# A GNN kernel whose opening is issued in another order, with two node tiles normalised by VectorE instead of ScalarE

## The chip, the cores and the metric

The kernel runs on one core of a Trainium2 chip. The metric is the device time of one execution in microseconds (us); smaller is better. The core's engines work side by side and meet at semaphores: TensorE (PE in the rows; PEld is its weight load), VectorE (DVE), ScalarE (ACT), GpSimd (POOL) and SyncE (SP), which here only issues transfers. An engine name with a q behind it (SPq, ACTq) is that engine's own sequencer, issuing a transfer. Each engine works off its own queue strictly in the order in which the program wrote it.

## What is computed

Four residual graph layers over N = 384 nodes with 1024 features. Each begins with the same step, and only the beginning of the first layer and the end of the last are touched here:

```python
h = jnp.maximum(_layernorm(x, axis=-1), 0.0)
x = x + attention(h, edges, edge_type_5)        # q = x @ wq.T + bq, k, v; q2 = q @ wiq.T + biq, ...; masked softmax
h = jnp.maximum(_layernorm(x, axis=-1), 0.0)
x = x + relational_conv(h, edges, edge_type_8)  # gated, 8 relations
h = jnp.maximum(_layernorm(x, axis=-1), 0.0)
x = x + sage(h, src, dst)                       # two layers
h = jnp.maximum(_layernorm(x, axis=-1), 0.0)
x = x + (h @ W.T + bias)                        # W scattered from (dst, src, edge_weight): 384 columns in use
```

`_layernorm(x)` is (x - mean) / sqrt(var + 1e-5). The mask of the attention comes from the 6144 edges: each (src, dst, type) writes a softplus of one of four edge weights into a 384 x 384 table, the last one winning.

## The kernel before

Nodes lie in NT = 3 tiles of P = 128 rows, features in KT = 8 blocks of 128. All products are made in split precision: each fp32 operand is turned into a high part (ScalarE's copy to fp32r, semaphores with "hi") and a low part (what is left, by VectorE's or GpSimd's subtraction, semaphores with "lo"), and each product is three matmuls. Everything is ordered by hand: each engine's block lists its instructions one by one, with waits on named semaphores.

The opening. SyncE loads the three tiles of x (`xres`, L280; semaphores x_part) and then the pieces of the first four tiles of wq (`raw`, L332). ScalarE issues the loads of src, dst and the two edge types (`e_in`, L903; semaphore edges_in, 16 for each). VectorE takes the statistics of each node tile: two bn_stats of 512 columns (L1262), then their aggregate (L1266). ScalarE takes the square root (`norm_std`, L910), VectorE the reciprocal and the shift -mean/std (`norm_shift`, L1275, L1276), and ScalarE normalises and applies the relu in one instruction (`norm_relu_0`, L933) into `h0`, with its columns permuted to go with the weights. `START` (L219) lists the work as (tile, first block, last block): tile 0, tile 1, and tile 2 in two halves. TensorE transposes each (L488) into PSUM, ScalarE reads it into the high part of `acts` (`start_high`, L941), VectorE makes the low part (`start_low`, L1355).

In between, VectorE makes four rows of the edges in `e_row` (L1289 to L1295): the key src * N + dst, its transpose, the type, and the key with the relation. The last one (L1295) gives `edge_rows`, for which SyncE waits to store the key rows (`rows_d`, L341) and to gather them broadcast to all partitions (`rows_b`, L285), and for which TensorE waits to turn them (`turn_edges`, L426) into PSUM bank 0; VectorE copies them out (`e_col`, L1363), and TensorE waits for that before it uses the bank again. GpSimd fills constants, then issues six loads of biases (`b_in`, L1789), which TensorE turns in one go (L493) and ScalarE copies (`bcol`, L998). Three small VectorE instructions (L1298 to L1300, `sp`) prepare the softplus, which ScalarE's L993 and L995 go on with.

The weights come by VectorE's transpose of 32 x 32 blocks (`turn_tile`, L1333, into `xres`, which is free by then), ScalarE's high part (`tile_high`, L954), and VectorE's low part (`tile_low`, L1337); weight tile 0's low part alone is made by GpSimd (L1794). A column tile (`column_tile`, L476) is 24 matmuls of 384 columns. It waits for its weight's low part, the first one also for `start_lo` up to 3 (tile 2's first half) and 4, and from the third on for the output two tiles before it to be read out of PSUM: high part L1005 by ScalarE, low part L1400 by VectorE (`out_lo`). Ahead of each L1400 VectorE makes two key comparisons (`meet`, L1310), which read the gathered rows.

The tail. In the last layer each node tile's sum is finished (L1735), its statistics taken, and it is normalised over its first 384 columns by ScalarE (L916), transposed by TensorE (L443), split (L926, L1325), and multiplied (nine matmuls, L892). VectorE adds the result to `u` (L1765), which GpSimd has made of x and the bias (L1946), and SyncE stores it.

## Time and profile before

| | us |
|---|---|
| median of 3 runs | 928.15 |
| lowest and highest | 927.82, 928.22 |
| the profiled execution | 927.87 |
| its span, first to last instruction | 926.1 |
| busy in the span: TensorE, VectorE, GpSimd, ScalarE | 906.8, 611.5, 492.3, 359.2 |

All rows are of the one profiled execution, with times in us from the start of its span. In a timeline a row is the start, how long it was busy, the engine, the line of the kernel, the operation, output <- inputs with partitions x elements, and a count where several were merged; behind it, in brackets, how long the engine sat idle before it and what released it. The granted clock of TensorE was 0.996 of full speed over the span. TensorE is busy nearly all the time, so the places to look at are those where it isn't yet, or not any more, fed without a gap: the first 29 us and the last 10.

### The profile page before, as it was taken

To read this page: it belongs to the slowest core of one execution; us is meant where nothing else is said; L and a number is where in the kernel's file an instruction comes from. 1 tells how busy PE (TensorE), PEld (TensorE's weight loads), DVE (VectorE), ACT (ScalarE), POOL (GpSimd) and SP (SyncE) were. 2 spreads that over 40 slices of the span, in tenths; PEclk is the share of its full clock that TensorE was granted. 3 is DMA by queue.
4 is the path that set the end of the run, shared out by engine and by line. 5 is a ranking of instruction groups with operands and counts; after the bars stand their busy time and mean duration, and the time that the engine had idled before them with its cause. 6 is when DMAs were issued, how large, how long until landed. Compare 5 with 4: busy or idle time off the path is not lost.

```text
span 926.1 us, 13755 instructions
## 1 busy us (share of the span) xinstructions
PE 906.8 (98%) x4787; PEld 799.0 (86%) x4787; DVE 611.5 (66%) x993; ACT 359.2 (39%) x558; POOL 492.3 (53%) x436
## 2 busy tenths in 40 slices
PE   4999999999999999999999999999999999999998
PEld 4999999998888888888888888888888878888886
DVE  6998888896996735665656565565656565434545
ACT  6433333345885343223223223232325235224422
POOL 5334446775765515757657575756686402220463
PEclk8999999999999999999999999999999999999999
DMA  8998756634336644344554444444333534323412
GB/s 207 241 277 224 229 155 151 167 85 119 53 52 204 178 155 146 92 151 114 152 152 130 153 113 150 113 148 111 97 91 137 182 98 154 114 93 91 140 42 91
DMA packets 89907, 128.60 MB, mean 139 GB/s; under 512 B 34480, under 2 KB 67456, under 8 KB 89856
## 3 DMA queue, kind: packets, MB, share of 16 engines
q1 hardware_dynamic: 72784, 123.54, 43.8%
q0 software_dynamic: 15552, 0.11, 4.0%
q10 hardware_dynamic: 1520, 4.30, 1.4%
q8 instruction: 29, 0.48, 0.2%
q14 instruction: 22, 0.18, 0.1%
HBM read 117.17 MB, written 7.59 MB: 135 GB/s over the span
## 4 chain that ended last, share of the span: by engine, by line
PE 90%; DVE 3%; ACT 2%; POOL 1%; DMA 1%; issue 1%; POOLq 0%; DVEq 0%; ACTq 0%
PE ps L682 49%; PE ps L476 17%; PE ps L756 9%; PE ps L520 4%; PE ps L645 4%; PE ps L600 2%; PE ps L543 2%; PE ps L556 2%; DMA weight_d<-weight_sum,cell 1%; PE ps L435 1%; POOL weight_d L1890 1%; PE ps L892 1%; DVE wlo_all L1388 1%; POOL mean_lo L1869 0%; PE ps L443 0%
## 5 line engine op out<-in xcount | busy, mean ns | idle before, releaser
L1388 DVE TENSOR_TENSOR wlo_all<-raw,whi_all 128x1024 fp32r<-128x1024 f32 x120 | 200.4, 1681 | 119.6 <-ACT whi_all L972 118.5
L476 PE MATMUL ps<-acts,whi_all 128*128 128x384 f32 (+1 forms) x640 | 164.1, 337 | 0.8 <-DVE acts L1400 0.6
L1869 POOL TENSOR_TENSOR mean_lo<-mean_f,mean_hi 128x384 fp32r<-128x384 f32 x76 | 88.3, 1162 | 120.4 <-ACT mean_hi L1124 120.4
L1124 ACT ACTIVATE mean_hi<-mean_f 128x384 fp32r<-128x384 f32 x76 | 39.9, 525 | 277.2 <-DVE mean_f L1562 277.2
L682 PE MATMUL ps<-whi_all,mean_hi 128*128 128x512 f32 x452 | 139.5, 390 | 0.3 <-POOL mean_lo L1869 0.3
L682 PE MATMUL ps<-wlo_all,mean_hi 128*128 128x512 f32 x452 | 139.3, 389 | 0.0
L682 PE MATMUL ps<-whi_all,mean_lo 128*128 128x512 f32 x452 | 139.3, 389 | 0.0
L972 ACT ACTIVATE whi_all<-raw 128x1024 fp32r<-128x1024 f32 x120 | 125.1, 1050 | 32.0 <-PE ps L682 28.5
L476 PEld LDWEIGHTS ps<-acts,whi_all 128*128 128x128 f32 x640 | 116.8, 190 | 1.2 <-DVE acts L1400 0.9
L1890 POOL DMA_INDIRECT weight_d<-weight_sum,cell x48 | 95.5, 1989 | 30.4 <-DMA weight_d<-weight_sum,cell 17.5
L476 PE MATMUL ps<-acts,wlo_all 128*128 128x384 f32 (+1 forms) x320 | 107.6, 336 | 0.0
L1833 POOL DMA_INDIRECT count_d<-met,cell x48 | 81.3, 1693 | 45.2 <-DMA count_d<-met,cell 32.0
L682 PEld LDWEIGHTS ps<-whi_all,mean_lo 128*128 128x128 f32 x452 | 84.9, 188 | 17.7
L682 PEld LDWEIGHTS ps<-wlo_all,mean_hi 128*128 128x128 f32 x452 | 84.9, 188 | 17.6
L682 PEld LDWEIGHTS ps<-whi_all,mean_hi 128*128 128x128 f32 x452 | 83.8, 188 | 12.6 <-issue 0.7
L1820 POOL DMA_INDIRECT mask_d<-type_val,cell x48 | 52.8, 1100 | 68.1 <-DMA mask_d<-type_val,cell 58.1
L1562 DVE TENSOR_TENSOR mean_f<-ps,inv 128x384 f32<-128x384 f32 x76 | 42.1, 554 | 60.5 <-PE ps L756 59.1
L1864 POOL TENSOR_TENSOR h_row_lo<-h,h_row_hi 128x1024 fp32r<-128x1024 f32 x9 | 24.6, 2756 | 99.1 <-ACT h_row_hi L1119 99.1
L756 PE MATMUL ps<-rel_r,h_row_lo 128*128 128x384 f32 x192 | 64.9, 338 | 0.0
L756 PE MATMUL ps<-rel_r,h_row_hi 128*128 128x384 f32 x192 | 64.9, 338 | 0.0
L1005 ACT ACTIVATE acts<-ps,bcol 128x384 f32 x40 | 23.3, 582 | 100.7 <-PE ps L476 87.9
L682 PE MATMUL ps<-whi_all,h_t_hi 128*128 128x512 f32 x192 | 60.8, 398 | 0.6 <-DVE wlo_all L1388 0.5
(211 smaller groups left out, 1705.6 us busy)
## 6 DMA issues: line engine op xcount, KB each, us to landing
raw<-in_L_gnn_weight SPq DMA_DIRECT2D x64, 512.0 KB
rows_b<-rows_d SPq DMA_DIRECT2D x24, 384.0 KB, 4.8
raw<-in_L_gnn_w_gate SPq DMA_DIRECT2D x16, 512.0 KB
raw<-in_L_gnn_W_self SPq DMA_DIRECT2D x16, 512.0 KB
raw<-in_L_gnn_W_neigh SPq DMA_DIRECT2D x16, 512.0 KB
count_d<-total_r SPq DMA_DIRECT2D x8, 576.0 KB
rel_r<-count_d SPq DMA_DIRECT2D x8, 576.0 KB, 4.5
raw<-in_L_gnn_wq SPq DMA_DIRECT2D x32, 128.0 KB
```

Source lines behind the costliest of these rows:

```text
L476: mm = pe.matmul(ps[:, j % 2, 0:N], stationary[j % RING][:, k, :], acts[:, a, moving, k, :], start=i == 0, stop=i == 3 * KT - 1)
L520: mm = pe.matmul(ps[:, V_BANK[n % 4], 0:V_COLS].rearrange("p (j o) -> p j o", j=2), acts[:, 3, a, k, P * nt:P * nt + P], weight[:, slots, ...
L682: mm = pe.matmul(ps[:, 2 * nt + f, :], stationary[a][:, k, P * nt:P * nt + P], weight[slot][:, HALF * f:HALF * f + HALF], start=first and ...
L756: mm = pe.matmul(ps[:, 7 - k % 2, 0:N], h_row[a][:, s, P * k:P * k + P], edges[:, s, :], start=i == 0, stop=i == 2 * NT - 1)
L972: act.activation(whi_row[slot], raw[slot][:, :], ACT.Copy).then_inc(S["w_hi"], 1)
L1124: act.activation(mean_of(q, k, 0)[:, 0, :], sums_of(q, k), ACT.Copy).then_inc(S["mean_hi"], 1)
L1388: dve.tensor_tensor(wlo_row[slot], raw[slot][:, :], whi_row[slot].bitcast(F32), ALU.subtract)\
L1562: dve.tensor_tensor(sums_of(q, k), ps[:, 7 - k % 2, 0:N], inv[:, :], ALU.mult)\
L1820: pool.indirect_dma_start(mask_d, bass.IndirectOffsetOnAxis(ap=cell[:, 0, c:c + 1], axis=0), type_val[:, c:c + 1], None).then_inc(mask_sca ...
L1833: pool.indirect_dma_start(count_d, bass.IndirectOffsetOnAxis(ap=cell[:, 1, c:c + 1], axis=0), met[:, 1, c:c + 1], None, compute_op=ALU.add)\
L1869: pool.tensor_tensor(mean_of(q, k, 1)[:, 0, :], sums_of(q, k), mean_of(q, k, 0)[:, 0, :].bitcast(F32), ALU.subtract).then_inc(S["mean_lo"], 1)
L1890: pool.indirect_dma_start(weight_d, bass.IndirectOffsetOnAxis(ap=cell[:, 2, c:c + 1], axis=0), weight_sum[:, c:c + 1], None, compute_op=AL ...
```

## The change

The opening, engine by engine:

- SyncE loads tile 0 of x in two halves of 512 columns, the first with a semaphore of its own, `x_half`.
- The four edge fields signal two semaphores, `ends_in` (src, dst) and `edges_in` (the types).
- VectorE takes each tile's stats as soon as its piece has landed, and does `norm_shift` of tile nt between the two halves of the stats of tile nt + 1. The two keys that need only src and dst are made behind tile 0's stats; the type row and the key with the relation (`edge_types`) only behind the low part of tile 0. Edge columns and the softplus's three small instructions are moved behind the last low part.
- Tile 2 is normalised by VectorE (`start_norm`, one tensor_scalar for each half, without the relu). The relu is applied where the transposed tile is read from PSUM: ScalarE's high part uses Relu for Copy, VectorE's low part is max(x, 0) - high in one scalar_tensor_tensor.
- ScalarE takes tile 2's square root ahead of tile 0's high part and has no normalisation of tile 2.
- TensorE turns the edges only after all node tiles, into bank 2 beside the biases, and doesn't wait for the edge columns any more; ScalarE does, before it copies `bcol`.
- GpSimd issues the six bias loads behind its first two instructions instead of behind its fills.

In the tail the last node tile is normalised by VectorE in the same way: a tensor_scalar of 384 columns, Relu for Copy in the high part, and max and subtract in the low part.

How the queues stand now. VectorE in the opening, from the shift of node tile 2 to the second weight transpose (L1333 or L1349), before (L1293 and L1295 make the type row and the key with the relation, L1363 the edge columns, L1298 to L1300 the softplus's first steps):

```order
L1276 TENSOR_SCALAR shift<-mv,rstd 128x1
L1293 CAST e_row<-e_in 48x128
L1295 SCALAR_TENSOR_TENSOR e_row<-e_in,e_row 48x128
L1298 TENSOR_SCALAR sp<-etw_b 128x4
L1299 TENSOR_SCALAR sp<-etw_b 128x4
L1300 TENSOR_TENSOR sp<-etw_b,sp 128x4
L1333 STREAM_TRANSPOSE xres<-raw 128x1024
L1355 TENSOR_TENSOR acts<-ps,acts 128x8x128
L1363 COPY e_col<-ps 128x192
L1355 TENSOR_TENSOR acts<-ps,acts 128x8x128
L1355 TENSOR_TENSOR acts<-ps,acts 128x4x128 x2
L1333 STREAM_TRANSPOSE xres<-raw 128x1024
```

and after (L1297 is the new normalisation, L1376 the low parts of tile 2; L1373 is L1355 of before):

```order
L1276 TENSOR_SCALAR shift<-mv,rstd 128x1
L1297 TENSOR_SCALAR h<-xres,rstd,shift 128x4x4x32 x2
L1373 TENSOR_TENSOR acts<-ps,acts 128x8x128
L1289 CAST e_row<-e_in 48x128
L1291 SCALAR_TENSOR_TENSOR e_row<-e_in,e_row 48x128
L1373 TENSOR_TENSOR acts<-ps,acts 128x8x128
L1376 SCALAR_TENSOR_TENSOR acts<-ps,acts 128x4x128 x2
L1391 COPY e_col<-ps 128x192
L1394 TENSOR_SCALAR sp<-etw_b 128x4
L1395 TENSOR_SCALAR sp<-etw_b 128x4
L1396 TENSOR_TENSOR sp<-etw_b,sp 128x4
L1349 STREAM_TRANSPOSE xres<-raw 128x1024
```

The type row and the key moved behind the low part of tile 0, the edge columns and the softplus behind all low parts, and the first weight transpose ahead of the shift.

ScalarE in the opening, from the first normalisation (L933, now L935) on; L910 (L912) is the square root, L941 (L943) a high part of a node tile, L954 (L956) one of a weight tile. Before:

```order
L933 ACTIVATE h<-xres,shift,rstd 128x4x8x32
L910 ACTIVATE std<-mv,epsc 128x1
L933 ACTIVATE h<-xres,shift,rstd 128x4x8x32
L941 ACTIVATE acts<-ps 128x8x128
L910 ACTIVATE std<-mv,epsc 128x1
L933 ACTIVATE h<-xres,shift,rstd 128x4x4x32 x2
L954 ACTIVATE whi_all<-xres 128x1024
L941 ACTIVATE acts<-ps 128x8x128
L941 ACTIVATE acts<-ps 128x4x128 x2
L954 ACTIVATE whi_all<-xres 128x1024
```

After:

```order
L935 ACTIVATE h<-xres,shift,rstd 128x4x8x32
L912 ACTIVATE std<-mv,epsc 128x1
L935 ACTIVATE h<-xres,shift,rstd 128x4x8x32
L912 ACTIVATE std<-mv,epsc 128x1
L943 ACTIVATE acts<-ps 128x8x128
L956 ACTIVATE whi_all<-xres 128x1024
L943 ACTIVATE acts<-ps 128x8x128
L943 ACTIVATE acts<-ps 128x4x128 x2
L956 ACTIVATE whi_all<-xres 128x1024
```

The normalisations of tile 2 are gone and its square root stands ahead of tile 0's high part.

VectorE in the tail, from the aggregate of the last tile's stats on, before:

```order
L1266 BN_AGGR mv<-stats 128x2
L1325 TENSOR_TENSOR h_t_lo<-ps,h_t_hi 128x3x128
L1275 RECIPROCAL rstd<-std 128x1
L1276 TENSOR_SCALAR shift<-mv,rstd 128x1
L1325 TENSOR_TENSOR h_t_lo<-ps,h_t_hi 128x3x128
L1765 TENSOR_TENSOR u<-u,ps 128x384 x3
```

and after:

```order
L1266 BN_AGGR mv<-stats 128x2
L1341 TENSOR_TENSOR h_t_lo<-ps,h_t_hi 128x3x128
L1275 RECIPROCAL rstd<-std 128x1
L1276 TENSOR_SCALAR shift<-mv,rstd 128x1
L1790 TENSOR_SCALAR h<-xres,rstd,shift 128x384
L1794 SCALAR_TENSOR_TENSOR h_t_lo<-ps,h_t_hi 128x3x128
L1802 TENSOR_TENSOR u<-u,ps 128x384 x3
```

The normalisation (L1790) has come in behind the shift, and the low part has become one scalar_tensor_tensor.

The diff, cut to its core:

```diff
@@ sync
-            for nt in range(NT):
+            sp_.dma_start(xres[:, 0, 0:HALF], x_rows[:, 0, 0:HALF]).then_inc(x_half, 16)
+            sp_.dma_start(xres[:, 0, HALF:D], x_rows[:, 0, HALF:D]).then_inc(x_part[0], 16)
+            for nt in range(1, NT):
                 sp_.dma_start(xres[:, nt, :], x_rows[:, nt, :]).then_inc(x_part[nt], 16)
@@ tensor
-                if n == 2:
-                    turn_edges()
...
+            pe.wait_ge(S["start_lo"], 1)
+            turn_edges()
             pe.wait_ge(S["bcol_in"], 16 * 6)
-            pe.wait_ge(S["start_lo"], 1)
             pe.transpose(ps[:, 2, 0:6 * KT], b_in[:, :], ident[0:6 * KT, 0:6 * KT]).then_inc(S["bcol_made"], 1)
-            pe.wait_ge(S["edge_cols"], 1)
@@ scalar
-                act.activation(acts[:, 0, 0, k0:k1, P * nt:P * nt + P], start_block(nt, k0, k1), ACT.Copy)\
-                   .then_inc(S["start_hi"], 1)
+                act.activation(acts[:, 0, 0, k0:k1, P * nt:P * nt + P], start_block(nt, k0, k1),
+                               ACT.Copy if nt < NT - 1 else ACT.Relu).then_inc(S["start_hi"], 1)
...
             norm_relu_0(*START[1])
+            norm_std(0, 2)
             start_high(0)
-            norm_std(0, 2)
-            norm_relu_0(*START[2])
-            norm_relu_0(*START[3])
             tile_high(0, 0)
...
             norm_std(3, 2)
-            norm_relu(3, 2, h, FIRST_THIRD)
-            tile_turned_high(Y_H3 + 2, 2, NT)
+            tile_turned_high(Y_H3 + 2, 2, NT, ACT.Relu)
@@ vector
+            def start_norm(nt, k0, k1):
+
+                dve.wait_ge(S["shift_ready"], nt + 1)
+                dve.tensor_scalar(h0[:, nt, :].rearrange("p (f b i) -> p b f i", f=KT, b=4)[:, :, k0:k1],
+                                  xres[:, nt, :].rearrange("p (b f i) -> p b f i", f=KT, b=4)[:, :, k0:k1],
+                                  rstd[:, nt, :], shift[:, nt, :], ALU.mult, ALU.add).then_inc(S["h_ready"], 1)
+
+            dve.wait_ge(x_half, 16)
+            half_stats(0, 0)
+            dve.wait_ge(x_part[0], 16)
+            half_stats(0, 1)
+            var_of(0, 0)
+            edge_keys()
+            dve.wait_ge(x_part[1], 16)
+            half_stats(1, 0)
+            norm_shift(0, 0)
+            half_stats(1, 1)
+            var_of(0, 1)
+            dve.wait_ge(x_part[2], 16)
+            half_stats(2, 0)
+            norm_shift(0, 1)
+            half_stats(2, 1)
+            var_of(0, 2)
...
             turn_tile(0, 0)
+            norm_shift(0, 2)
+            start_norm(*START[2])
+            start_norm(*START[3])
             start_low(0)
-            dve.wait_ge(S["edges_turned"], 1)
-            dve.tensor_copy(e_col[:, :, :], ps[:, 0, 0:4 * EC].rearrange("p (f c) -> p f c", f=4))\
-               .then_inc(S["edge_cols"], 1)
+            edge_types()
             start_low(1)
             start_low(2)
             start_low(3)
+            dve.wait_ge(S["edges_turned"], 1)
+            dve.wait_ge(S["bcol_made"], 1)
+            dve.tensor_copy(e_col[:, :, :], ps[:, 2, P:P + 4 * EC].rearrange("p (f c) -> p f c", f=4))\
+               .then_inc(S["edge_cols"], 1)
...
-            tile_turned_low(Y_H3 + 2, 2, NT)
+            dve.wait_ge(S["shift_ready"], NT * 4)
+            dve.tensor_scalar(h[:, NT - 1, 0:N], xres[:, NT - 1, 0:N], rstd[:, NT - 1, :], shift[:, NT - 1, :],
+                              ALU.mult, ALU.add).then_inc(S["h_ready"], 1)
...
@@ gpsimd
+            for g, b in enumerate((bq, bk, bv, biq, bik, biv)):
+                pool.dma_start(b_in[KT * g:KT * g + KT, :].rearrange("j (c o) -> j c o", c=4) if g < 3
...
             pool.memset(total_r[:, :, :].bitcast(F32), 0.0).then_inc(S["zeros_made"], 1)
```

## Rows read from the trace of the kernel before

**Rows 1.** Engines' busy time over the span, from the page: us, share, instructions.
```profile
PE 906.8 (98%) x4787; PEld 799.0 (86%) x4787; DVE 611.5 (66%) x993; ACT 359.2 (39%) x558; POOL 492.3 (53%) x436
```

**Rows 2.** VectorE in the timeline of the opening: start us, us, engine, line, operation.
```profile
8.72 1.28 DVE L1262 BATCH_NORM_STATS2 stats<-xres 128x6 f32<-128x512 f32 x2
...
11.69 0.28 DVE L1295 SCALAR_TENSOR_TENSOR e_row<-e_in,e_row 48x128 f32<-48x128 int32 x1
11.89 0.15 DVE L1298 TENSOR_SCALAR sp<-etw_b 128x4 f32<-128x4 f32 x1
...
12.38 1.25 DVE L1333 STREAM_TRANSPOSE xres<-raw 128x1024 f32<-128x1024 f32 x1
...
13.55 1.19 DVE L1355 TENSOR_TENSOR acts<-ps,acts 128x1024 fp32r<-128x1024 f32 x1
...
14.66 0.34 DVE L1363 COPY e_col<-ps 128x192 f32<-128x192 f32 x1
...
15.66 2.42 DVE L1355 TENSOR_TENSOR acts<-ps,acts 128x1024 fp32r<-128x1024 f32 x3 [0.66 <-ACT acts L941]
...
17.99 1.24 DVE L1333 STREAM_TRANSPOSE xres<-raw 128x1024 f32<-128x1024 f32 x1
```

**Rows 3.** ScalarE and GpSimd in the same timeline.
```profile
8.84 1.24 ACT L933 ACTIVATE h<-xres,shift,rstd 128x1024 f32<-128x1024 f32 x1 [0.48 <-DVE shift L1276]
...
9.99 1.02 ACT L941 ACTIVATE acts<-ps 128x1024 fp32r<-128x1024 f32 x1
...
13.66 1.06 ACT L954 ACTIVATE whi_all<-xres 128x1024 fp32r<-128x1024 f32 x1 [0.46 <-DVE xres L1333]
...
14.80 2.36 POOL L1794 TENSOR_TENSOR wlo_all<-xres,whi_all 128x1024 fp32r<-128x1024 f32 x1 [4.59 <-ACT whi_all L954]
...
17.12 1.01 POOL L1799 TENSOR_TENSOR moved<-e_col,spare 128x48 f32<-128x48 f32 x3
```

**Rows 4.** Timelines of TensorE and VectorE, first and third column tile.
```profile
17.63 0.98 PE L476 MATMUL ps<-acts,whi_all 128*128 128x384 f32 x2 [0.21 <-DVE acts L1355]
...
27.90 0.61 DVE L1400 SCALAR_TENSOR_TENSOR acts<-ps,bcol,acts 128x384 fp32r<-128x384 f32 x1
...
28.57 0.61 PE L476 MATMUL ps<-acts,whi_all 128*128 128x384 f32 x2 [0.57 <-DVE acts L1400]
```

**Rows 5.** Tile view of xres, transfers: ns and start; time to landing.
```profile
L280 SPq DMA_DIRECT2D xres<-in_x x3: 394/415/424, 0.8 to 1.7; - x3
...
DMA to landing us min/median/max: 3.4/4.4/6.7
```

**Rows 6.** Timeline at 702 of GpSimd and VectorE; L1388's durations.
```profile
701.84 2.40 POOL L1930 TENSOR_TENSOR rows_b<-rows_b,h 128x1024 f32<-128x1024 f32 x1 [7.14 <-DMA brow<-in_L_gnn_b_gate]
...
702.16 3.17 DVE L1388 TENSOR_TENSOR wlo_all<-raw,whi_all 128x1024 fp32r<-128x1024 f32 x1 [2.09 <-ACT whi_all L972]
...
L1388 DVE TENSOR_TENSOR wlo_all<-raw,whi_all x120: 1171/1226/3908, 311.9 to 899.2; 128x1024 fp32r<-128x1024 f32 x120
```

**Rows 7.** Timeline of the tail, all engines.
```profile
917.26 2.40 POOL L1946 TENSOR_TENSOR u<-xres,brow 128x1024 f32<-128x1024 f32 x1 [1.99 <-DVE xres L1735]
...
918.71 0.21 DVE L1276 TENSOR_SCALAR shift<-mv,rstd 128x1 f32<-128x1 f32 x1
...
918.96 0.71 ACT L916 ACTIVATE h<-xres,shift,rstd 128x384 f32<-128x384 f32 x1 [0.48 <-DVE shift L1276]
919.08 0.68 PE L892 MATMUL ps<-w_hi,h_t_lo 128*128 128x384 f32 x3
...
919.72 0.55 PE L443 MATMUL ps<-ident,h 128*128 128x128 f32 x3
```

**Rows 8.** SyncE's key rows: timeline; transfers with size and time to landing.
```profile
11.99 0.31 SPq L341 DMA_DIRECT2D rows_d<-e_row  x1
...
rows_b<-rows_d SPq DMA_DIRECT2D x3, 384.0 KB, 5.0
...
rows_d<-e_row SPq DMA_DIRECT2D x1, 48.0 KB, 6.2
```

More of the change, by code:

```diff
@@ L425, in turn_edges @@
                 for f in range(4):
-                    mm = pe.transpose(ps[:, 0, EC * f:EC * f + EC], e_row[:, f, :], ident[0:EC, 0:EC])
+                    mm = pe.transpose(ps[:, 2, P + EC * f:P + EC * f + EC], e_row[:, f, :], ident[0:EC, 0:EC])
                 mm.then_inc(S["edges_turned"], 1)
@@ L1277, in norm_shift @@
                    .then_inc(S["shift_ready"], 1)
-            def start_stats(nt):
-                dve.wait_ge(x_part[nt], 16)
-                norm_stats(0, nt)
-            for nt in range(NT):
-                start_stats(nt)
-                if nt < NT - 1:
-                    norm_shift(0, nt)
-            dve.wait_ge(S["edges_in"], 16 * 4)
-            dve.scalar_tensor_tensor(e_row[:, KEY, :], e_in[:, 0, :], float(N), e_in[:, 1, :], ALU.mult, ALU.add)\
-               .then_inc(S["key_made"], 1)
@@ L1291, in _ @@
-            dve.scalar_tensor_tensor(e_row[:, KEY_T, :], e_in[:, 1, :], float(N), e_in[:, 0, :], ALU.mult, ALU.add)
-            norm_shift(0, NT - 1)
-            dve.tensor_copy(e_row[:, TYPE, :], e_in[:, 3, :])
-            dve.wait_ge(S["key_made"], 1)
-            dve.scalar_tensor_tensor(e_row[:, REL_KEY, :], e_in[:, 2, :], float(N * N), e_row[:, KEY, :],
-                                     ALU.mult, ALU.add).then_inc(S["edge_rows"], 1)
-            dve.wait_ge(S["etw_in"], 16)
-            link(dve.tensor_scalar(sp[:, 0, :], etw_b[:, :], 0.0, None, ALU.max))
@@ L1299, in _, with edge_keys @@
-            link(dve.tensor_scalar(sp[:, 1, :], etw_b[:, :], -1.0, None, ALU.mult))
-            dve.tensor_tensor(sp[:, 2, :], etw_b[:, :], sp[:, 1, :], ALU.max).then_inc(S["sp_max"], 1)
+            def edge_keys():
+                dve.wait_ge(S["ends_in"], 16 * 2)
+                dve.scalar_tensor_tensor(e_row[:, KEY, :], e_in[:, 0, :], float(N), e_in[:, 1, :], ALU.mult, ALU.add)\
+                   .then_inc(S["key_made"], 1)
+                dve.scalar_tensor_tensor(e_row[:, KEY_T, :], e_in[:, 1, :], float(N), e_in[:, 0, :], ALU.mult, ALU.add)
@@ new lines, in edge_types @@
+            def edge_types():
+                dve.wait_ge(S["edges_in"], 16 * 2)
+                dve.tensor_copy(e_row[:, TYPE, :], e_in[:, 3, :])
+                dve.wait_ge(S["key_made"], 1)
+                dve.scalar_tensor_tensor(e_row[:, REL_KEY, :], e_in[:, 2, :], float(N * N), e_row[:, KEY, :],
+                                         ALU.mult, ALU.add).then_inc(S["edge_rows"], 1)
+            def start_norm(nt, k0, k1):
[3 more added lines that the diff above has]
+                                  rstd[:, nt, :], shift[:, nt, :], ALU.mult, ALU.add).then_inc(S["h_ready"], 1)
@@ L1354, in start_low @@
                 dve.wait_ge(S["start_hi"], n + 1)
[L1355 to L1357 removed]
+                low, high = [acts[:, 0, a, k0:k1, P * nt:P * nt + P] for a in (1, 0)]
+                if nt < NT - 1:
+                    dve.tensor_tensor(low, start_block(nt, k0, k1), high.bitcast(F32), ALU.subtract)\
+                       .then_inc(S["start_lo"], 1)
+                else:
+                    dve.scalar_tensor_tensor(low, start_block(nt, k0, k1), 0.0, high.bitcast(F32), ALU.max,
+                                             ALU.subtract).then_inc(S["start_lo"], 1)
             dve.wait_ge(S["h_ready"], 1)
             turn_tile(0, 0)
+            norm_shift(0, 2)
+            start_norm(*START[2])
+            start_norm(*START[3])
             start_low(0)
[L1362 to L1364 removed]
+            edge_types()
             start_low(1)
```

32 lines of the change are left out of this document (20 added, 12 removed).

## The prediction

> **What bounds the kernel now.** I read the page's first part first: TensorE is busy 98% of the span [rows 1]. In such a kernel a change to the opening or to the tail counts only through the moment from which TensorE never waits again, and through what follows its last matmul. So I looked next for TensorE's last long wait in the opening. It is the third column tile of the first projection: its first matmul starts at 28.57 after 0.57 us of idle time, released by VectorE's L1400, which started at 27.90 [rows 4]. TensorE had begun its first column tile at 17.63 [rows 4], so an earlier beginning of that tile alone only makes the 0.57 us of waiting longer. What counts is the chain of VectorE from the second weight transpose (17.99, [rows 2]) to that L1400. I call the start of that transpose T. All that stands between T and L1400 (two more transposes, two low parts, the softplus of the edge weights by way of ScalarE, the mask blocks, two key comparisons) is in the same order before and after, so L1400 moves with T, one to one. This holds as long as TensorE ends its second column tile, 0.57 us ahead of the wait, before L1400 is there.
>
> The tail is a single chain as well: shift of node tile 2 on VectorE, normalisation on ScalarE (0.71 us), transposes on TensorE, and the last nine matmuls [rows 7].
>
> **Part 1, x in halves and the stats in another order.** Three transfers of x are issued at 0.8 to 1.7; their times to landing are 3.4, 4.4 and 6.7 us, so tile 2 lands at about 1.7 + 6.7 = 8.4 [rows 5]. Before, VectorE reaches tile 2's stats at 8.72 [rows 2] and finds them landed. In the new order VectorE does tile 0 by about 5.2, the two key rows (some 0.45), tile 1 by about 7.6, and then waits for tile 2. So what half a tile of x gains is lost at once to the landing of tile 2; I take 8.43 for the start of its stats (0.3 earlier than before). It could be 0.4 later, since one more issue of 0.42 stands ahead of it [rows 5], or a little sooner; the whole opening then moves with it.
>
> Behind the first half of the stats (0.6) come reciprocal and shift of tile 1 (0.4), now at 9.44, where before ScalarE could start on that tile at 8.84 [rows 3]. So ScalarE normalises tile 1 at 9.5, 0.6 later. It then has the square root of tile 2 (10.65, since L941 follows L933 by 1.15), the high part of tile 0 (10.85 to 11.85, its 1.02) and the high part of weight tile 0 at 11.85 to 12.9, in place of 13.66 to 14.72 [rows 3]. That is the gain of this part: ScalarE no longer normalises tile 2 ahead of the weight. GpSimd's low part of weight tile 0 (2.36) follows at 12.95 and ends at 15.3, where before it ran from 14.80 to 17.16 [rows 3].
>
> **Part 2, VectorE between there and T.** After the last stats (10.3): transpose 1.17 from its start to the next [rows 2], reciprocal and shift 0.4, so 11.85; the two halves of tile 2, normalised. No row shows a tensor_scalar of 512 elements from SBUF to SBUF; the bounds are 0.27 (half of the stats' 0.6, less what is fixed in it) and 0.60 (the spacing of the 512-element stats [rows 2]). It doesn't matter which, as will be seen. They end at 12.4 to 13.0. Low part of tile 0 (1.19 [rows 2]): to 13.5 or 14.1. And then comes the moved part: the cast of the types and the key with the relation (e_row<-e_in,e_row). Before, these ran at 11.69 [rows 2], with GpSimd idle. Now they come at 13.5 to 14.1, in the middle of GpSimd's low part of the weight (12.95 to 15.3). That key instruction reads two operands in SBUF, as GpSimd's does. What such a pair does is seen at 702: VectorE's L1388, also with two SBUF operands, starts at 702.16, takes 3.17 us (their median is 1.23) and ends 1.1 us after GpSimd's L1930 has ended at 704.24 [rows 6]. It waited for GpSimd's instruction to end. I expect the same here: the key instruction starts at 15.3, and all of VectorE's queue stands behind it (the low parts of tiles 1 and 2, the edge columns, the softplus, T). The Trainium skill says the same, in SBUF — State Buffer, section "Who interferes with whom": a VectorE instruction with two SBUF inputs contends with a GpSimd one that reads SBUF, and the second blocks wholly; by that rule, which the row at 702 bears out, the sum stays as it is.
>
> From there: key 0.2, low part of tile 1 from 15.5, then 1.13 and twice 0.6 (15.66 to 17.99 before, [rows 2]), which gives 17.85. Then the two pieces that used to stand ahead: edge columns 0.3, and the three small softplus instructions 0.49 (11.89 to 12.38, [rows 2]): T = 18.65. The softplus ones now run beside GpSimd's three L1799 (1.01 in all, starting right behind the edge columns; [rows 3]). They may wait for each other: 0 to 0.6, and I take 0.2. T = 18.85 against 17.99: **0.85 us later**. The low part of tile 2's first half ends at about 17.3, so TensorE starts its column tile at 17.4 instead of 17.6, which buys nothing.
>
> **Part 3, the b_in transfers issued first, and turned edges in bank 2.** GpSimd's six issues move ahead of its fills, which end later by as much, still before its low part of the weight can start; the first to read a fill is VectorE, behind T. The biases, issued some microseconds sooner, are no longer the last to arrive. Cost and gain nothing; their cover is that VectorE's low parts end last. The turned edges (0.5 us of TensorE) now follow the key at 15.6 and are ready at 16.3, with the bias transpose at 16.6; VectorE wants them at 17.85. If TensorE were 1.2 us later there, this would begin to cost.
>
> **Part 4, the tail.** Before: shift ends 918.92, ScalarE normalises 918.96 to 919.67, TensorE transposes at 919.72 [rows 7]. TensorE itself is busy with tile 1's product: its last group of three starts at 919.08 at 0.17 each [rows 7], so it could take the transposes at 919.6 and no sooner. The new VectorE instruction (384 elements) would be ready at 918.96 and take 0.27 to 0.46, so the gain is capped at 0.12. The other bound: GpSimd's L1946 runs from 917.26 to 919.66 [rows 7]. If VectorE waits for it as at 702, it starts at 919.6 and ends at 919.9 to 920.1, a loss of 0.2 to 0.4. No row shows a VectorE instruction with one SBUF operand beside a long one of GpSimd; the nearest that shows anything is the elementwise L1388, which waits. I take that side: **+0.25**. The Trainium skill (same page, same section) lists tensor_scalar among the operations that can use both ports and so contend with GpSimd; by it the tail would lose, and without it gain 0.12. The relu is done while reading PSUM, at the price of the copy. TensorE's nine last matmuls and the store are the same.
>
> **Sum.** +0.85 + 0.25 = +1.1 us. The profiled execution took 927.87, which gives 929.0; the median of the runs is 0.28 above it, and on that base I predict **929.2**. That is 0.12%, below the 0.2% (1.9 us) that a measurement of this kernel can tell from no change.
>
> **Rivals.**
> *No wait in the opening*: the key instruction (48 partitions only) passes beside GpSimd. Then the low part of tile 1 starts when ScalarE's high part of it is there, 13.85, or up to 14.3 with the slower normalisation, and T = that + 3.15 = 17.0 to 17.45: 0.55 to 1.0 us earlier. TensorE's own chain, begun 0.9 or more earlier too, does not take its place. With the tail at -0.1 to +0.25: 927.0 to 927.9, likeliest 927.4. For it: it is a third as many partitions and an eighth as many elements as L1388, and no row shows so small a one beside a long one of GpSimd. Against it: the row at 702. Chance 0.27.
> *Slower by more than 0.2%*: the stored key rows. SyncE stores them at 11.99, it takes 6.2 us to land, and the gather behind it 5.0 [rows 8]. Now the store can't be issued before 15.6; if it still takes 6.2, the gather is issued at 21.9 and lands at 26.9; the first comparison, one of two that take 0.9 together right ahead of L1400 (27.90, [rows 4]), was at 27.0 and is due at 27.9. The margin is 1.0. For it: the whole SyncE queue, raw tiles too, stands behind. Against: before, the store waited behind sixteen weight pieces on its queue, and those are nearly done at 15.6. If the gather took 7 instead of 5, the comparison would be 1.0 late: 929.2 + 1.0 = 930.2; the gather at 7.5 gives 930.7. Chance 0.11.
> *Faster by more than 0.2%*: needs no wait in the opening and tile 2 of x a full microsecond sooner. Chance 0.04.
>
> **How the numbers follow.** The forecast has 0.58, with its own range 928.6 to 929.9 (tile 2 of x 0.4 later; softplus 0 to 0.6; tail from -0.1 to +0.4). No wait 0.27, slower 0.11, faster 0.04. The range 926.9 to 930.3 holds the forecast, the no-wait case and the near part of the slow one. Faster 0.04, same 0.84, slower 0.12.
>
> **What would show it.** VectorE's stats of tile 2 wait for the transfer until 8.4; GpSimd's low part of the weight runs from 13.0 to 15.3; the key or the cast before it shows a duration of 1 to 2 us and ends at 15.3 to 15.6; the second weight transpose starts at 18.6 to 19.3; TensorE idles 1.3 us or more ahead of its third column tile, released by the same product at 29.2 to 29.7; the VectorE normalisation at 918.9 ends only after GpSimd's addition. I am wrong if the key shows 0.28 us, or if the second transpose starts before 17.9, or if the first comparison waits for a transfer.

## The result, and the profile after

The changed kernel takes **932.58 us** (median of 7 runs, lowest 932.28), the kernel before 927.85 (median of 7 runs beside them): ratio 1.0058, 95% interval [1.0044, 1.0073]. Slower by 0.58%, outside the predicted range (926.9 to 930.3), whose middle case was 929.2. The profiled execution of the changed kernel took 932.28, its span is 930.5 against 926.1. Of most kernels here, the one before included, some executions take 2 to 9 us longer than the rest, so medians are compared.

VectorE, ScalarE and GpSimd in the timeline of the opening of the changed kernel (start us, us, engine, line, operation; in brackets the idle time before and what ended it). Its lines are numbered up to 37 higher than those of the kernel before. The rows answer to [rows 2, 3]:

```profile
9.04 0.69 DVE L1262 BATCH_NORM_STATS2 stats<-xres 128x6 f32<-128x512 f32 x1 [2.91 <-DMA xres<-in_x]
...
11.38 0.69 DVE L1262 BATCH_NORM_STATS2 stats<-xres 128x6 f32<-128x512 f32 x1 [0.49 <-DMA xres<-in_x]
...
14.09 1.25 DVE L1349 STREAM_TRANSPOSE xres<-raw 128x1024 f32<-128x1024 f32 x1 [0.86 <-DMA raw<-in_L_gnn_wq]
...
15.66 1.01 DVE L1297 TENSOR_SCALAR h<-xres,rstd,shift 128x512 f32<-128x512 f32 x2
...
17.72 1.26 DVE L1289 CAST e_row<-e_in 48x128 f32<-48x128 int32 x1
18.90 0.28 DVE L1291 SCALAR_TENSOR_TENSOR e_row<-e_in,e_row 48x128 f32<-48x128 int32 x1
...
22.27 1.25 DVE L1349 STREAM_TRANSPOSE xres<-raw 128x1024 f32<-128x1024 f32 x1
...
15.37 1.06 ACT L956 ACTIVATE whi_all<-xres 128x1024 fp32r<-128x1024 f32 x1 [0.61 <-DVE xres L1349]
...
16.51 2.39 POOL L1831 TENSOR_TENSOR wlo_all<-xres,whi_all 128x1024 fp32r<-128x1024 f32 x1 [5.83 <-ACT whi_all L956]
21.85 1.03 POOL L1836 TENSOR_TENSOR moved<-e_col,spare 128x48 f32<-128x48 f32 x3 [2.96 <-DVE e_col L1391]
```

Three things are to be seen. The statistics of node tile 1 (9.04) and of tile 2 (11.38) wait for their transfers, 2.91 and 0.49 us. The first weight transpose (14.09) waits 0.86 for its tile. And the cast of the types, 0.21 us before, lasts from 17.72 to 18.98, until GpSimd's low part of the weight (16.51 + 2.39 = 18.90) has ended. The second weight transpose, T, starts at 22.27 in place of 17.99: **4.28 us later**.

TensorE's waits in the opening and the last row of the tail (answering to [rows 4, 7]):

```profile
21.05 0.98 PE L479 MATMUL ps<-acts,whi_all 128*128 128x384 f32 x2 [0.99 <-DVE acts L1376]
...
32.85 0.62 PE L479 MATMUL ps<-acts,whi_all 128*128 128x384 f32 x2 [0.66 <-DVE acts L1429]
...
32.19 0.60 DVE L1429 SCALAR_TENSOR_TENSOR acts<-ps,bcol,acts 128x384 fp32r<-128x384 f32 x1
...
921.46 2.40 POOL L1983 TENSOR_TENSOR u<-xres,brow 128x1024 f32<-128x1024 f32 x1 [1.99 <-DVE xres L1764]
...
922.91 0.21 DVE L1276 TENSOR_SCALAR shift<-mv,rstd 128x1 f32<-128x1 f32 x1
...
923.16 0.92 DVE L1790 TENSOR_SCALAR h<-xres,rstd,shift 128x384 f32<-128x384 f32 x1
...
924.71 0.49 ACT L928 ACTIVATE h_t_hi<-ps 128x384 fp32r<-128x384 f32 x1 [2.04 <-PE ps L446]
```

The product that releases the third column tile starts at 32.19 instead of 27.90: 4.29 later, as T. In the tail the normalisation of 384 elements lasts 0.92 us beside GpSimd's L1983, and from the shift's start to the high part pass 1.80 us, where it was 1.60 in the kernel before (918.71 [rows 7] to 920.31, its row below): +0.2. The two together are 4.5; the span grew by 4.4.

```profile
920.31 0.49 ACT L926 ACTIVATE h_t_hi<-ps 128x384 fp32r<-128x384 f32 x1 [0.64 <-PE ps L443]
```

### The profile page after: what moved, and what is told of

Its sections match the earlier page's. It is cut to its first block, busy times and chain, and to the rows that moved or that the text cites. A ratio compares the mean times of both kernels' runs of the same rounds, so it can differ in the third digit from the quotient of the medians.

```text
span 930.5 us, 13757 instructions
## 1 busy us (share of the span) xinstructions
PE 908.6 (98%) x4787; PEld 800.6 (86%) x4787; DVE 613.7 (66%) x996; ACT 357.0 (38%) x555; POOL 493.5 (53%) x436
## 4 chain that ended last, share of the span: by engine, by line
PE 89%; DVE 4%; DMA 2%; ACT 1%; POOL 1%; issue 1%; SPq 0%; DVEq 0%; POOLq 0%; ACTq 0%
PE ps L683 49%; PE ps L479 17%; PE ps L757 9%; PE ps L521 4%; PE ps L646 4%; PE ps L601 2%; PE ps L544 2%; PE ps L557 2%; DMA raw<-in_L_gnn_wq 1%; DMA weight_d<-weight_sum,cell 1%; PE ps L438 1%; POOL weight_d L1927 1%; DVE wlo_all L1417 1%; POOL mean_lo L1906 0%; PE ps L467 0%
## 5 line engine op out<-in xcount | busy, mean ns | idle before, releaser
L1857 POOL DMA_INDIRECT mask_d<-type_val,cell x48 | 56.0, 1166 | 65.6 <-DMA mask_d<-type_val,cell 55.6
```

The source lines that it names most:

```text
L1857: pool.indirect_dma_start(mask_d, bass.IndirectOffsetOnAxis(ap=cell[:, 0, c:c + 1], axis=0), type_val[:, c:c + 1], None).then_inc(mask_sca ...
```

## The experiments

All runs stand against 21 to 35 runs of the kernel before, 927.92 to 927.96 in the median. T is read from each profile; between two profiles of one opening it differed by 0.48 us (`a_whole` and its second look, 19.97 and 19.49) and by 0.11 (`a_types` and `a_types_fill`, 20.22 and 20.11). The three suspects in the opening are tile 0 of x in two transfers, the bias loads ahead of GpSimd's fills, and the place of the casts.

### First four: the transfers

`a_bin_late`, the changed kernel with the bias loads back behind the fills:

```diff
-            for g, b in enumerate((bq, bk, bv, biq, bik, biv)):   # ahead of memset(total_r)
...
+            for g, b in enumerate((bq, bk, bv, biq, bik, biv)):   # ahead of wait_ge(S["w_hi"], 1)
```

> The changed kernel with one part undone: GpSimd's six bias loads issued behind its fills, as before. Theory A (the early bias loads disturb the x loads, whose second and third tile landed 3 us late): the stats of tile 1 start by 6.0 and those of tile 2 at 8.4 to 8.8; the waits on GpSimd's low part stay, so the time is 929.0 to 929.8. Theory B (x in two halves is what delays the tiles): no change, 932.3 to 932.8, tile 2's stats at 11.4.

`a_whole`, tile 0 of x in one transfer again:

```diff
-            sp_.dma_start(xres[:, 0, 0:HALF], x_rows[:, 0, 0:HALF]).then_inc(x_half, 16)
-            sp_.dma_start(xres[:, 0, HALF:D], x_rows[:, 0, HALF:D]).then_inc(x_part[0], 16)
-            for nt in range(1, NT):
+            for nt in range(NT):
```

> The changed kernel with tile 0 of x loaded whole again, the bias loads still early. Theory A: as the changed kernel, 932.3 to 932.8, tile 2's stats at 11.0 to 11.4. Theory B: tile 1's stats by 6.0, tile 2's at 8.4, time 929.0 to 929.8.

`a_both`, both edits at once:

> The changed kernel with both undone: tile 0 of x whole and the bias loads behind the fills. Both theories: x as in the kernel before (tile 2's stats at 8.4 to 8.7); what is left over the kernel before is the waiting of VectorE for GpSimd's low part of the weight (0.85 us forecast) and the tail (0.2): 928.9 to 929.4. If the whole excess were the transfers': 927.9 or less.

`b_bin_early`, the kernel before with the bias loads ahead of the fills:

> The kernel before with one part of the change alone: the six bias loads issued ahead of GpSimd's fills. Theory A: tile 1's stats start near 9 and tile 2's near 11.4, and the time rises by 2 to 3 us, to 930 to 931. Theory B: 927.8 to 928.2, as before.

Measured, with T and the span of the profiled execution:

| kernel | median us | ratio, 95% interval | T | span |
|---|---|---|---|---|
| before | 927.96 | | 17.99 | 926.1 |
| a_bin_late | 931.81 | 1.0044 [1.0027, 1.0061] | 21.04 | 929.4 |
| a_whole | 932.4, see below | 1.0047 [1.0030, 1.0064] | 19.97 | 928.4 |
| a_both | 929.89 | 1.0036 [1.0021, 1.0051] | 19.14 | 927.5 |
| b_bin_early | 927.97 | 1.0000 [0.9990, 1.0009] | 18.09 | 926.4 |

VectorE in the timeline of `a_bin_late`:

```profile
8.26 0.69 DVE L1262 BATCH_NORM_STATS2 stats<-xres 128x6 f32<-128x512 f32 x1 [2.42 <-DMA xres<-in_x]
...
10.88 0.69 DVE L1262 BATCH_NORM_STATS2 stats<-xres 128x6 f32<-128x512 f32 x1 [0.77 <-DMA xres<-in_x]
...
12.72 1.25 DVE L1349 STREAM_TRANSPOSE xres<-raw 128x1024 f32<-128x1024 f32 x1
```

and in that of `a_whole`:

```profile
6.01 0.68 DVE L1260 BATCH_NORM_STATS2 stats<-xres 128x6 f32<-128x512 f32 x1
...
8.75 0.69 DVE L1260 BATCH_NORM_STATS2 stats<-xres 128x6 f32<-128x512 f32 x1 [0.91 <-DMA xres<-in_x]
...
11.78 1.25 DVE L1346 STREAM_TRANSPOSE xres<-raw 128x1024 f32<-128x1024 f32 x1 [1.19 <-DMA raw<-in_L_gnn_wq]
```

With the halves kept, tiles 1 and 2 still come late (8.26, 10.88); with tile 0 in one transfer tile 1 is there at 6.01 and tile 2 at 8.75. The bias loads are not the cause of that. They may be a smaller one: without them at the front T is 1.23 earlier with the halves kept and 0.83 (against the second profile 0.35) with x whole, and the first weight tile is there sooner (transpose at 12.72 without a wait, against 14.09 with 0.86). The 1.23 is more than T's own scatter and agrees with the times (931.81 against 932.58). With x whole the difference is within the scatter, and both kernels take about 929.6 apart from their long executions, so there it isn't shown. In the kernel before, where VectorE comes to that tile only at 12.38 [rows 2], they change nothing.

`a_both` showed a second thing, in the timelines of VectorE and GpSimd:

```profile
5.63 0.23 DVE L1280 SCALAR_TENSOR_TENSOR e_row<-e_in 48x128 f32<-48x128 int32 x1
5.79 1.24 DVE L1282 SCALAR_TENSOR_TENSOR e_row<-e_in 48x128 f32<-48x128 int32 x1
...
4.45 1.06 POOL L1819 MEMSET mask<- 128x1152 f32 x1
5.58 1.30 POOL L1820 TENSOR_SCALAR_AFFINE_SELECT mask<-mask 128x1152 f32<-128x1152 f32 x1
```

The key's second instruction, 0.28 us in the changed kernel and beside a memset, takes 1.24 us beside GpSimd's affine_select, which reads SBUF, and ends 0.15 us behind it. The first one (5.63) started only 0.05 us behind the affine_select and wasn't held: it took its usual 0.23, and the affine_select 1.30 where it takes 1.16 in the kernel before. The key's wait costs little here, since tile 2's statistics start at 8.71, as in `a_whole` (8.75). The 929.89 lie above the 928.9 to 929.4 that both theories gave; four of its nine runs are long ones (931.35 and more), the other five lie between 929.28 and 929.89.

### Next four: one part alone

`b_halves`, the kernel before with nothing but tile 0 of x in two transfers:

```diff
-            for nt in range(NT):
+            sp_.dma_start(xres[:, 0, 0:HALF], x_rows[:, 0, 0:HALF]).then_inc(x_half, 16)
+            sp_.dma_start(xres[:, 0, HALF:D], x_rows[:, 0, HALF:D]).then_inc(x_part[0], 16)
+            for nt in range(1, NT):
                 sp_.dma_start(xres[:, nt, :], x_rows[:, nt, :]).then_inc(x_part[nt], 16)
```

> The kernel before with one edit: tile 0 of x comes in two transfers, its stats wait for both. Theory 'halves delay the tiles behind them': tiles 1 and 2 of x land about 3 us later (stats of tile 2 at 11 instead of 8.72 us), T from 17.99 to 20.3 or later, time 930.3 or more, ratio 1.0025 or more. Rival 'it needs the changed order too' (the delay in the changed kernel came from the other loads of the opening and chance): stats of tile 2 at 8.7 to 9.3, time 927.9 to 928.4.

Measured: **930.39 us**, 1.0017 [1.0004, 1.0031], T = 20.71, 2.72 later; span 928.8 (+2.7). VectorE's timeline:

```profile
9.25 1.29 DVE L1265 BATCH_NORM_STATS2 stats<-xres 128x6 f32<-128x512 f32 x2 [2.18 <-DMA xres<-in_x]
...
11.49 1.29 DVE L1265 BATCH_NORM_STATS2 stats<-xres 128x6 f32<-128x512 f32 x2
...
20.71 1.23 DVE L1338 STREAM_TRANSPOSE xres<-raw 128x1024 f32<-128x1024 f32 x1
```

Tile 1's statistics start at 9.25 after 2.18 us of waiting, tile 2's at 11.49 in place of 8.72 [rows 2]. The theory stands, in the kernel before as well: the halves alone cost 2.4 us of median.

Two things about it can be read from the traces. The core's 16 DMA engines moved less in the first microseconds: from 3 to 5 us they ran at 404 GB/s in the kernel before, at 208 in `b_halves` and at 245 in the changed kernel; over all profiles it is 391 to 406 with tile 0 in one transfer and 208 to 286 with halves. The rates in 40 slices of 0.65 us from 0 to 26, first of the kernel before, then of the changed one:

```profile
GB/s 0 0 32 191 407 404 415 359 323 333 232 79 137 275 301 232 228 227 226 223 219 225 229 227 199 151 43 0 0 85 288 169 301 295 213 169 252 407 350 217
GB/s 0 0 22 236 378 309 80 301 349 314 379 240 144 300 222 207 249 224 230 246 210 252 199 254 214 178 61 22 22 0 30 46 0 47 269 154 293 281 224 164
```

And tile 2 was overtaken: by the start of its statistics 1.95 MB had been moved in the kernel before (8.72 us at 224 GB/s) and 2.49 MB in the changed one (11.38 at 219), so by this estimate some 0.5 MB more of other loads went first, weight pieces queued behind it for the most part (edges and biases together are 0.12 MB). Whether the shorter rows (2 KB instead of 4) or the additional transfer is the reason was not tested.

`a_types`, the changed kernel with the casts moved right behind the last variance:

```diff
             half_stats(2, 1)
             var_of(0, 2)
+            edge_types()
...
             start_low(0)
-            edge_types()
```

> The changed kernel with the cast of the edge types and their relation key alone moved right behind the last variance (13.2 us in its profile, where VectorE waited 0.86 us for the weight tile, so that they cost nothing there). Theory 'two parts that add up': x in halves keeps its 2.6 us, GpSimd's wait of 1.38 us (17.72 to 19.10) goes: T from 22.27 to 20.9, time 932.58 - 1.4 = 931.2 us, ratio 1.0035. Rival 'the wait hides behind something else', for instance ScalarE's high part of tile 1, which ended at about 17.2: T stays at 22 or above, time 932.2 to 932.6.

`a_both_types`, the same move on top of `a_both`:

> The changed kernel with tile 0 of x in one transfer, the bias loads back behind GpSimd's fills, and the casts of the edge types with their relation key moved right behind the last variance, ahead of GpSimd's low part of the weight. The same without that last move started the second weight transpose (T) at 19.14, with the cast of 1.39 us inside GpSimd's 2.36 us. Theory 'GpSimd makes VectorE wait': cast 0.2 us, low part of tile 1 directly behind that of tile 0, T = 19.14 - 1.52 + 0 = 17.6, third column tile 0.3 earlier than in the kernel before, tail +0.2: 927.8 us, ratio 0.9998. Rival 'the low part of tile 1 is bound by ScalarE's high part anyway': T stays above 18.5, time 928.9 or more. Second question, open: the two runs with x whole scattered by up to 5 us; if this comes from TensorE's clock rising late (it begins the first column tile late after a broken row of short transposes), it goes on here or shrinks with T; if from the cast and what it delays, it is gone and all runs lie within 0.5 us.

Measured: `a_types` 931.47 us, 1.0033 [1.0017, 1.0049], T = 20.22; `a_both_types` 929.04 us, 1.0015 [0.9999, 1.0031], T = 18.92. In `a_types` the cast is back at its size:

```profile
12.86 0.16 DVE L1289 CAST e_row<-e_in 48x128 f32<-48x128 int32 x1
...
13.41 1.25 DVE L1350 STREAM_TRANSPOSE xres<-raw 128x1024 f32<-128x1024 f32 x1 [0.19 <-ACT h L935]
...
20.22 1.25 DVE L1350 STREAM_TRANSPOSE xres<-raw 128x1024 f32<-128x1024 f32 x1
```

T is 2.05 earlier: 1.38 from the cast, 0.68 from the first weight transpose, which starts sooner in this execution (13.41 instead of 14.09). The time fell by 1.1 and the span by 0.4 only. In `a_both_types` the move brought 0.22 instead of 1.52, and neither theory had the reason. The first weight transpose starts at 11.23 instead of 10.81, and above all: with the bias loads late, VectorE's edge columns now wait 0.79 for TensorE's transpose of the biases, which waited 2.17 for b_in.

```profile
18.05 0.36 DVE L1388 COPY e_col<-ps 128x192 f32<-128x192 f32 x1 [0.79 <-PE ps L493]
...
17.61 0.34 PE L493 MATMUL ps<-ident,b_in 48*128 48x48 f32 x1 [2.17 <-DMA b_in<-in_L_gnn_biv]
```

So the two moves of the change depend on each other: early casts need early biases. The second question of that expectation got a plain answer: the scatter went on without the wait (928.62 to 933.39).

`b_tail`, the kernel before with the change of the tail alone (the ScalarE and VectorE lines of the tail in the diff above):

> The kernel before with the change of the tail alone: node tile 2 of the last norm normalised by VectorE, relu while reading PSUM. Theory 'VectorE waits for GpSimd's addition': the normalisation of 384 elements lasts until GpSimd's 2.40 us instruction has ended, from shift to high part 1.59 us instead of 1.39, time 927.96 + 0.2 = 928.2 us, ratio 1.0002. Rival 'the end of the kernel is timed by something else': no difference, 927.96. Rival 'the scatter of the changed kernel comes from the tail': runs here scatter by 1 us and more; by the first theory they lie within 0.5 us.

Measured: 928.23 us against 927.96, 1.0011 [0.9992, 1.0030]: the 0.2 us can't be told from nothing by the ratio, the median sits where it was expected, and the profile has the 0.92 us again. That all runs would lie within 0.5 us was wrong: three of eleven took 931.03, 932.63 and 934.89.

### Last four: what was left over

Why did T fall by 2.05 in `a_types`, but the span by 0.4? TensorE in its timeline, and the windows behind it (the columns of the windows: stretch, length, busy us of PE, PEld, DVE, ACT, POOL, granted clock, DMA share, GB/s):

```profile
30.80 0.62 PE L479 MATMUL ps<-acts,whi_all 128*128 128x384 f32 x2 [2.36 <-DVE acts L1429]
31.25 0.49 PE L479 MATMUL ps<-acts,wlo_all 128*128 128x384 f32 x1
...
28.00:30.00 2.00, 0.44 (x3) 0.12 (x1) 2.00 (x5) 1.53 (x2) 1.81 (x3) 1.00 0.99 325
...
32.00:34.00 2.00, 2.00 (x8) 2.00 (x7) 2.00 (x6) 0.99 (x1) 0.20 (x1) 0.50 1.14 217
```

Here TensorE had run its first column tile at full pace (0.17 us a matmul from the first; the kernel before and the changed one take 0.98 for the first two [rows 4] and 0.32 for each up to 21.6 and 26.6), so it was done early, stood idle for 2.36 us ahead of the third, and behind that wait the granted clock was 0.50, its 1.2 GHz level: 0.32 us a matmul instead of 0.17, from 31.25 to 34.9. Some eleven matmuls lose 0.15 each, 1.6 us in all, with no wait left to hide it. `a_types_fill` puts eight matmuls into that wait:

```diff
                 for j in range(first, KT):
+                    if isinstance(g, int) and (g, j) == (0, 2):
+                        for _ in range(8):
+                            pe.matmul(ps[:, 3, 0:N], whi[1][:, 0, :], acts[:, a, 0, 0, :], start=True, stop=True)
```

> The kernel with the edge types early (931.47 us), and in TensorE's wait ahead of the third column tile (28.4 to 30.80 us in its profile) eight matmuls more of 128x384 into an unused bank, about 1.4 us of work; they add work whose result nobody reads. In that profile TensorE ran the first two column tiles at 0.17 us a matmul, waited 2.36 us, and then ran 31.3 to 34.7 at 0.32 us a matmul with a granted clock of 0.50: about 1.7 us lost with no wait left to hide it. Theory 'the idle time lets the clock fall': with about 1 us left of the wait there is no half-rate stretch behind it, third column tile at 30.8 as before, 931.5 - 1.7 = 929.8 us. Rival 'the clock falls there whatever TensorE did': the half-rate stretch stays, 931.5 us. Where an execution runs its first column tile at half rate, the eight matmuls end after the wait and cost up to 1.3 us.

Measured: 930.66 us, 1.0029 [1.0015, 1.0043], 0.8 below `a_types`, with runs from 928.81; in the profile 0.95 us of waiting is left and no half-rate stretch behind it (0.33 at once):

```profile
30.69 0.62 PE L479 MATMUL ps<-acts,whi_all 128*128 128x384 f32 x2 [0.95 <-DVE acts L1432]
31.15 0.34 PE L479 MATMUL ps<-acts,wlo_all 128*128 128x384 f32 x1
```

That supports the theory that TensorE's idle time let its clock fall; in the other profiles that show a wait at that place, 0.51 to 1.65 us, no half-rate stretch follows. It rests on one profile of each, the gain in the median is half of the 1.7 expected, and the runs of the two kernels overlap (929.39 to 934.76 against 928.81 to 936.44), so the gain in time is not shown, and in how many executions this stretch occurs stays open.

`a_whole_look` looked at `a_whole` again for its scatter:

> The kernel with tile 0 of x in one transfer, looked at once more, for its scatter: its runs were 929.4, 929.8, 930.1 and 932.4, 933.6, 934.3, 934.4 us. The profile so far is of a 930.1 run, with the first column tile at half rate (19.5 to 23.4) and no half-rate stretch behind TensorE's wait. Theory 'TensorE's clock falls in another place': a profile of 932 or more shows matmuls of 0.32 us behind the wait ahead of the third column tile or later, for 4 to 7 us, with T at 20.0. Rival 'the transfers vary': it shows T later by as much as the time.

It gave 929.56 us in the median, seven of eight runs from 929.47 to 930.05 and one of 933.89, 1.0019 [1.0002, 1.0036]. So a_whole's own time is 929.6, and its 932.4 above came from four long runs in seven. The profiled execution was a short one and shows neither theory. An answer came from the profiled execution of `a_types_fill`, itself a long one (936.44 us). Its waits ahead of the first score tiles of the attention, 200 us behind the opening (engine, line waited for, total us, times, longest), the windows there, and the transfer that is waited for:

```profile
DVE sc_more L1453 <- DMA mask<-mask_d: 8.4, 1, 8.4
...
PE ps L547 <- DVE nmax L1453: 3.7, 1, 3.7
...
215.00:220.00 5.00, 1.76 (x15) 1.55 (x13) 0.69 (x3) 0.08 (x1) 1.56 (x1) 0.88 0.82 247
220.00:225.00 5.00, 4.59 (x21) 4.15 (x22) 3.89 (x17) 3.07 (x11) 1.56 (x1) 0.50 1.05 397
...
215.17 0.39 SPq L377 DMA_DIRECT2D mask<-mask_d  x1
```

The same transfer in the timeline of the kernel before:

```profile
204.27 0.39 SPq L374 DMA_DIRECT2D mask<-mask_d  x1
```

The mask table is filled first, by a chain of 48 indirect stores of GpSimd. In this execution the table's reload was issued at 215.17 instead of 204.27, VectorE waited 8.43 us for it, TensorE 3.7, and behind that wait the granted clock was 0.50 from 220 to 225. In `a_both_types` and in `a_whole_look` the reload was 4.3 us late for VectorE, and TensorE did not notice. The kernel before has the same chain and had long runs too, but few: 3 of 96 lie more than 2 us above its fastest (930.73, 933.60, 933.78), against 4 of 9 in `a_both`, 5 of 15 in `a_whole` and its second look, and 3 of 11 in `b_tail`, whose opening is that of before. The reload also starts later in every profile of the changed opening (205.4 to 210.4, in the long one 215.2) than in the kernel before and those with its opening and x whole (204.2 to 204.5) or in `a_best` (203.9). So the change may make such runs more frequent; that isn't settled, nor that all of them are of this kind: one was caught.

`a_best`, the changed opening mended (x whole, biases early, casts and softplus pieces early, their lines below taken out) with the tail of before:

```diff
             var_of(0, 2)
+            edge_types()
+            dve.wait_ge(S["etw_in"], 16)
+            link(dve.tensor_scalar(sp[:, 0, :], etw_b[:, :], 0.0, None, ALU.max))
+            link(dve.tensor_scalar(sp[:, 1, :], etw_b[:, :], -1.0, None, ALU.mult))
+            dve.tensor_tensor(sp[:, 2, :], etw_b[:, :], sp[:, 1, :], ALU.max).then_inc(S["sp_max"], 1)
```

> The changed opening mended: tile 0 of x in one transfer, types, relation key and softplus pieces right behind the last variance, ahead of GpSimd's low part of the weight; and the tail of the kernel before. The first weight tile lands at about 11.8 us (as with x whole and biases early); from there transpose, shift, normalisation 0.92, low parts 1.14, 1.14, 1.2, edge columns: T at about 18.0, as in the kernel before (17.99). Theory 'the two waits and the tail explain the loss': 927.7 to 928.2 us. Rival 'TensorE has the last word': it starts its first column tile 1 us later than in the kernel before or with a longer wait ahead of the third, and its clock costs 1 to 2 us: 929 or more, with a half-rate stretch behind that wait.

Measured: **927.84 us**, 1.0001 [0.9991, 1.0010], T = 17.58, span 925.7: the loss is gone, and no more than that. VectorE and GpSimd:

```profile
9.73 1.02 DVE L1288 CAST e_row<-e_in 48x128 f32<-48x128 int32 x1
...
11.37 1.25 DVE L1352 STREAM_TRANSPOSE xres<-raw 128x1024 f32<-128x1024 f32 x1
...
17.58 1.23 DVE L1352 STREAM_TRANSPOSE xres<-raw 128x1024 f32<-128x1024 f32 x1
...
9.52 1.16 POOL L1818 TENSOR_SCALAR_AFFINE_SELECT mask<-mask 128x1152 f32<-128x1152 f32 x1
```

Even here the cast meets a GpSimd instruction that reads SBUF (9.52 to 10.68) and lasts until just behind its end (10.75).

`b_tail_free`, `b_tail` with GpSimd's last addition held until the normalisation is done:

```diff
                 pool.wait_ge(S["x_done"], 2 * nt + 2)
+                if nt == NT - 1:
+                    pool.wait_ge(S["h_ready"], H_ALL[3] + 3)
```

> The kernel before with the new tail, and GpSimd's last addition (2.40 us, 917.14 in the profile of the tail alone) held until VectorE's normalisation of node tile 2 is done. Theory 'VectorE waits for GpSimd's addition': the normalisation takes 0.3 to 0.5 us instead of 0.92, the transposes start about 0.4 us earlier, 928.23 - 0.4 = 927.8 us, a shade below the kernel before (927.96). Rival 'VectorE needs 0.9 for 384 elements anyway': 0.92 again, 928.2. Rival 'the last addition becomes the end': it ends at 921.5 and its store of 640 columns lands last, 928.5 or more.

Measured: 929.53 us, 1.0027 [1.0012, 1.0042]. The first theory holds in its mechanism, the last rival in the time. The normalisation takes 0.48 us:

```profile
919.05 0.48 DVE L1760 TENSOR_SCALAR h<-xres,rstd,shift 128x384 f32<-128x384 f32 x1
...
919.67 2.38 POOL L1955 TENSOR_TENSOR u<-xres,brow 128x1024 f32<-128x1024 f32 x1 [4.32 <-DVE h L1760]
...
922.65 0.55 DVE L1772 TENSOR_TENSOR u<-u,ps 128x384 f32<-128x384 f32 x1 [0.43 <-PE ps L892]
```

and VectorE's last instruction starts at 922.65, in `b_tail` at 922.84; counted from the shift (918.80 and 918.59) that is 0.4 earlier. But the addition ends at 922.05; its 320 KB per store stand in SyncE's queue ahead of the last two, and the span ends 4.6 us behind VectorE's last instruction in place of 2.8.

## Right and wrong, step by step

**Part 1, the failed step: "I take 8.43 for the start of its stats".** Tile 2's statistics start at 11.38, 2.95 later than forecast, because tile 0 in two transfers makes tiles 1 and 2 land late. The prediction took the times to landing of three whole tiles [rows 5] for those of two halves and two tiles, and allowed 0.4 for one issue more. `b_halves` shows the price by itself: T 2.72 later, 2.4 us of time. That halves could slow down what stands behind them was no rival of the prediction at all, so its range ended too low.

**Between there and GpSimd's low part.** Forecast 15.3 - 8.43 = 6.9 us from the start of tile 2's statistics to the end of GpSimd's instruction, measured 18.90 - 11.38 = 7.5. The 0.65 more is the wait for the first weight tile, which the prediction did not have. Early bias loads may add to it (1.23 in T with the halves kept, from one profile each), so "Cost and gain nothing" in part 3 is doubtful for the changed kernel, though right for the kernel before.

**Part 2, the wait for GpSimd.** Right in its mechanism and place. The instruction that waits is already the cast, with one operand, and it needs 1.26 instead of 0.21. The key behind it shows its 0.28, which the prediction had named as a sign of being wrong; it isn't one, because the cast ahead of it had done the waiting, as the sentence before that sign allowed. With the casts moved away the wait is gone. From GpSimd's end to T the forecast had 3.55, measured 3.37 (the softplus pieces lost 0.1 and not 0.2). The rival without a wait is refuted by the same row, and by `a_both`'s 1.39.

The sum, corrected: 0.85 + 2.95 + 0.65 - 0.18 = 4.27, measured 4.28.

**T passes to the end one to one.** Right: T and the product move by 4.28 and 4.29. In the profiles the span follows T plus 0.1 to 0.35 for the new tail: the changed kernel +4.28 and +4.4, `a_bin_late` +3.05 and +3.3, `a_both` +1.15 and +1.4, `a_both_types` +0.93 and +1.2, `a_whole` +1.98 and +2.3; with the old tail `b_halves` +2.72 and +2.7, `a_best` -0.41 and -0.4. The exception is `a_types` (+2.23 and +4.0), where TensorE's clock adds its 1.6.

**Part 3, turned edges.** Their transposes cost nothing in the changed kernel, as forecast; the limit given there (TensorE 1.2 us later would begin to cost) was reached in `a_both_types`, by the biases.

**Part 4, the tail.** Forecast +0.25, measured +0.20 in the profile and +0.27 in the median of `b_tail`, where the interval does not exclude zero. `b_tail_free` shows its cause: 0.44 of the 0.92 us are waiting. The Trainium skill's rule (SBUF — State Buffer, section "Who interferes with whom"), that tensor_scalar and cast can use both port pairs and then contend with GpSimd, agrees with the 1.26 and the 0.92. That a VectorE instruction with two SBUF inputs contends only with a GpSimd instruction that reads SBUF (same page and section of the Trainium skill) agrees with the key's 0.28 beside a memset and 1.24 beside an affine_select.

**The slower rival** had the right sign and the wrong mechanism: the stored key rows landed 1.6 us after their issue, not 6.2, and no comparison waited for them.

## What to carry to other kernels

Splitting a load so that its first half can be used sooner also moves everything queued behind it: here 0.5 us were to be gained on tile 0, and the statistics of tiles 1 and 2 started 3 us later. Before splitting, ask which of the transfers is the last one wanted, and price a split by a run, not by the landing times of whole transfers. When a VectorE instruction is moved, look what GpSimd does at its new time: a cast of 48 x 128 that came while a GpSimd instruction reading SBUF was under way lasted until that one had ended, in each of the five kernels where it did so.
